# A Mamba and mixture-of-experts layer on one core: the places of its side work fitted anew

## The chip, the cores and the metric

The kernel runs on one core of a Trainium2 chip. The time is the device time of one execution in microseconds (us). Three executions of the kernel before took 4769.98, 4778.06 and 4780.16 us; the median is 4778.06. The engines are PE (TensorE), DVE (VectorE), ACT (ScalarE), POOL (GpSimd) and SP (SyncE, which here only issues transfers). Each runs its own list of instructions in order and waits on semaphores for the others.

## What is computed

```python
x = x + layernorm(mamba(layernorm(x)))        # x: 8 sequences, 1024 tokens, 256 channels
x = x + layernorm(moe(layernorm(x)))

# mamba, once forward and once on the reversed sequence, 512 channels, 16 states:
h = exp(delta * A) * h + (delta * B * x)       # one step a token
y = sum over states of h * C, + D * x, * silu(z)
# the two directions are added, halved, and go through W_out
# moe: a shared expert, and for each token the 2 best of 8 experts, gelu(t @ w1 + b1) @ w2 + b2
```

## The kernel before

The eight sequences are eight blocks. A block has two waves: w = 2b is the forward direction, w = 2b + 1 the backward one. A wave has 16 states times 4 groups of 128 channels, so 64 units, and the whole program 1024. A unit is one scan over 1024 tokens: ACT makes `decay` (PSUM, two buffers) with an Exp of `delta`, POOL makes `drive` (three buffers) from `xu` and a row of B, DVE scans both into `h`. PE transposes `h` into `h_t` by tiles of 128 tokens, and each tile is multiplied with C and added into `y`: twelve of sixteen tiles on DVE (L1118), four as `scaled` on ACT (L1328) and a sum on POOL (L1574).

The main loop of each engine goes over slots, two to a unit. In an even slot DVE does a scan, in each slot it may add one tile, and behind that come the pieces of side work whose place falls into the slot. A place is a number in the table AT, sixteen to a slot:

```python
def put(self, engine, at, piece, *index):
    self.slots[engine, at // PARTS].append((at, piece, index))
```

So slot 1024 is unit 512, the first of block 4. A slot is no time: an engine works its list as fast as its waits allow. Nothing checks that a piece that makes something stands in an earlier slot than the one that uses it on another engine; the semaphore then holds the second one up, and with it all that stands behind it on its engine.

The pieces of side work fall into three chains. *Preparing the next wave*: tok_load, norm, proj, xz_copy, the convolution as tap0 (ACT, L1357) and tap (DVE, L1181, three operations), silu_x (L1362), dbc_mm, then for each channel group c dt_mm, softplus (ACT, L1404 to L1408), delta (DVE, L1148), u_mul (POOL, L1588), delta_store and delta_load through DRAM (SP, L1756 and L1762). The `decay` of a wave's units of group c needs its delta_load. The backward wave's input comes back by xz_load (L1723), which waits for the last delta of the forward wave, as both use one buffer. *Finishing the block before*: y_dump, y_load (L1789), z_mm, z_copy and z_silu (L1420), y_turn, y_add, gate, out_mm, norms, residual. *Its experts*: routing on DVE (top1, top2, `slots`), scatter of the tokens on POOL (L1619, 16 indirect transfers for a block), for groups of four blocks of 128 tokens xs_load, xs_turn, r1_mm (L1073), r1_copy (L1518), a GELU (rgelu, L1524), r2_mm (L1081), ys_copy (L1536), ys_store (L1865), then gather on POOL (L1630, 16 transfers), comb_mm (L1058), comb (L1280), and the last norm: statistics, `ln_rstd` on POOL, ln_apply on ACT (L1449), fin_add (L1286), out_store. The experts of a block reach over the next block's units and into the one after; the gather stands at the start of that.

The side work's PSUM products share two banks. A second table, BANK_USE, numbers the uses; even numbers are one bank, odd ones the other, and a product waits for the piece that empties the use two numbers before it.

SP's list holds all hardware transfers in order, so one that waits holds up those behind it.

Of the kernel before, what the change touches and what calls it, by code (L numbers as in the profile page):

```python
# [1944 lines left out]
```

## Time and profile before

| | us |
|---|---|
| median of three executions | 4778.06 |
| the profiled execution | 4797.45 |
| its span | 4796.2 |
| before the first scan | 105.0 |
| scans, 1024 units | 4279.6 |
| from the last scan's start to the end | 411.5 |

The profiled execution is one of its own, so sums are made against its 4797.45. Busy shares of its span: DVE 83%, POOL 74%, PE 72%, ACT 62%. In the trace a row names the line of the program, the engine, what it writes and reads by the program's buffer names, and in square brackets how long the engine had stood idle before it and what ended that.

### The profile page before, as it was taken

The page shows a single profiled execution, that of the slowest core. Times are in us where ns is not written, and L with a number is a line of the kernel's source. Part 1 is how long each engine was busy: PE and PEld are TensorE (multiplying, and loading weights), DVE is VectorE, ACT ScalarE, POOL GpSimd, SP SyncE. Part 2 cuts the span into 40 slices and gives each one's busy share as a digit, 9 for nine tenths or more (in the row PEclk, how much of TensorE's full clock was granted, in tenths as well). Part 3 has the DMA queues.
Part 4 walks back from the last instruction along what each step waited for, and adds up shares of the span by engine and source line. Part 5 has one row for each costly group of instructions (what it writes and reads, how often), then busy time and mean ns, then how long its engine had stood idle before and what let it go on. Part 6 is the DMA issues. An engine that isn't in the chain of part 4 may idle for free.

```text
span 4796.2 us, 52660 instructions
## 1 busy us (share of the span) xinstructions
PE 3453.1 (72%) x16720; PEld 2505.7 (52%) x16720; DVE 3984.6 (83%) x4136; ACT 2979.6 (62%) x4196; POOL 3571.5 (74%) x2119
## 2 busy tenths in 40 slices
PE   4466767786777867887678867787678867787575
PEld 1344444665446644665456644566456655565354
DVE  2999998998989889799998989899997989896200
ACT  3454655775657756676657856677566756575243
POOL 2798887978877878778888878878887878786111
PEclk7565777998879878898779977898779988798687
DMA  4321331555325543456325543356424554255144
GB/s 130 106 79 66 110 128 71 184 180 178 129 96 189 180 152 120 144 184 204 129 91 176 196 157 132 123 179 215 142 84 166 174 194 137 94 186 162 62 157 148
DMA packets 362016, 687.42 MB, mean 143 GB/s; under 512 B 31873, under 2 KB 205450, under 8 KB 357642
## 3 DMA queue, kind: packets, MB, share of 16 engines
q1 hardware_dynamic: 349450, 650.48, 40.9%
q0 software_dynamic: 12288, 33.57, 2.2%
q8 instruction: 133, 2.18, 0.2%
q14 instruction: 145, 1.19, 0.1%
HBM read 513.04 MB, written 170.92 MB: 143 GB/s over the span
## 4 chain that ended last, share of the span: by engine, by line
DVE 31%; issue 18%; PE 17%; POOL 13%; ACT 12%; DMA 8%; SPq 1%; DVEq 0%; POOLq 0%; ACTq 0%
DVE h L1103 14%; DVE y L1118 9%; POOL drive L1566 7%; PE h_t L946 4%; PE side L1081 3%; DVE side L1181 3%; ACT decay L1310 2%; PE side L1051 2%; DMA expert_w<-in_w 2%; POOL y L1574 2%; POOL work L1630 2%; DVE stats L1162 1%; DMA ys_dram<-work 1%; PE side L1073 1%; DMA dx_dram<-prep_work 1%
## 5 line engine op out<-in xcount | busy, mean ns | idle before, releaser
L1566 POOL TENSOR_TENSOR drive<-xu,b_row 128x1024 f32<-128x1024 f32 x1024 | 2408.6, 2364 | 298.7 <-DVE h L1103 295.1
L1103 DVE TENSOR_TENSOR_SCAN h<-decay,drive 128x1024 f32<-128x1024 f32 x1024 | 2334.0, 2279 | 127.4 <-POOL drive L1566 85.4
L946 PE MATMUL h_t<-ident,h 128*128 128x128 f32 x8192 | 1511.2, 324 | 770.7 <-DVE y L1118 483.2
L946 PEld LDWEIGHTS h_t<-ident,h 128*128 128x128 f32 x8192 | 1128.0, 166 | 1261.0 <-DVE y L1118 714.0
L1310 ACT ACTIVATE decay<-delta,neg_a 128x1024 f32<-128x1024 f32 x1024 | 1141.5, 1117 | 789.6 <-DVE h L1103 736.9
L1118 DVE SCALAR_TENSOR_TENSOR y<-h_t,c_col,y 128x512 f32<-128x512 f32 x1488 | 1071.4, 734 | 147.8 <-PE h_t L946 139.0
L1574 POOL TENSOR_TENSOR y<-y,scaled 128x512 f32<-128x512 f32 x496 | 632.1, 1274 | 320.5 <-ACT scaled L1328 317.2
L1073 PE MATMUL side<-xn_t,expert_w 128*128 128x128 f32 x2944 | 415.3, 288 | 95.0 <-DMA expert_w<-in_w 26.7
L1081 PE MATMUL side<-expert_w,work 128*128 128x256 f32 x1472 | 405.3, 428 | 47.4 <-issue 29.6
L1073 PEld LDWEIGHTS side<-xn_t,expert_w 128*128 128x128 f32 x2944 | 378.2, 202 | 113.1 <-ACT work L1536 31.0
L1328 ACT ACTIVATE scaled<-h_t,c_col 128x512 f32<-128x512 f32 x496 | 339.8, 685 | 113.6 <-PE h_t L946 111.1
L1081 PEld LDWEIGHTS side<-expert_w,work 128*128 128x128 f32 x1472 | 307.0, 218 | 106.1 <-issue 38.0
L1630 POOL DMA_INDIRECT work<-ys_dram,slot_i x128 | 123.8, 967 | 254.7 <-DMA ys_dram<-work 224.3
L1280 DVE TENSOR_TENSOR acc<-side,acc 128x512 f32<-128x512 f32 x32 | 22.1, 690 | 287.4 <-PE side L1058 283.3
L1518 ACT ACTIVATE work<-side,b_blocks 128x128 f32<-128x128 f32 x736 | 208.1, 365 | 63.4 <-PE side L1073 63.1
L1181 DVE SCALAR_TENSOR_TENSOR side<-prep_work,chan_sb,side 128x512 f32<-128x512 f32 x256 | 191.8, 749 | 38.9 <-ACT side L1357 34.2
L1619 POOL DMA_INDIRECT xs_dram<-work,slot_i x128 | 125.5, 980 | 127.6 <-DVE owner_hot L1274 67.3
L1588 POOL TENSOR_TENSOR xu<-xu,prep_work 128x1024 f32<-128x1024 f32 x64 | 151.0, 2359 | 81.9 <-DVE prep_work L1148 81.6
L1058 PE MATMUL side<-work 128*128 128x256 f32 x256 | 113.9, 592 | 112.1 <-DMA work<-ys_dram,slot_i 85.8
L984 PE MATMUL side<-dbc,wdt_sb 97*128 97x512 f32 x256 | 171.8, 785 | 18.6 <-DVE prep_work L1148 9.0
L1051 PE MATMUL side<-expert_w,work 128*128 128x256 f32 x512 | 152.0, 450 | 35.7 <-ACT work L1472 31.4
L964 PE MATMUL side<-xn_t,w_in_sb 128*128 128x512 f32 x256 | 139.8, 677 | 28.6 <-DVE xu L1181 26.1
(148 smaller groups left out, 3730.0 us busy)
## 6 DMA issues: line engine op xcount, KB each, us to landing
expert_w<-in_w SPq DMA_DIRECT2D x384, 512.0 KB, 4.1
b_row<-b_dram SPq DMA_DIRECT2D x256, 512.0 KB, 4.4
dx_dram<-prep_work SPq DMA_DIRECT2D x64, 512.0 KB, 3.4
delta_dram<-prep_work SPq DMA_DIRECT2D x64, 512.0 KB
delta<-delta_dram SPq DMA_DIRECT2D x64, 512.0 KB, 3.6
work<-xs_dram SPq DMA_DIRECT2D x40, 512.0 KB, 4.8
ys_dram<-work SPq DMA_DIRECT2D x40, 512.0 KB, 5.4
xz_dram<-prep_work SPq DMA_DIRECT2D x32, 512.0 KB, 4.1
```

Source lines behind the costliest of these rows:

```text
L946: t = pe.e.transpose(h_t[i % N_H_T][:, c * P:(c + 1) * P], h[:, gn % 2, c, tb * P:(tb + 1) * P], ident[:, :])
L1051: pe.e.matmul(o, h1[:, m, q * P:(q + 1) * P], wo[:, m, :], start=(m == 0), stop=False)
L1073: mm = pe.e.matmul(bank[:, m * P:(m + 1) * P], wi[:, k, m * P:(m + 1) * P], xn2_t[:, k, at:at + P], start=(k == 0), stop=(k == DC - 1))
L1081: mm = pe.e.matmul(bank[:, q % 2 * D:(q % 2 + 1) * D], h1_blocks[:, q, m, :], wo[:, m, :], start=(m == 0), stop=(m == HC - 1))
L1103: dve.e.tensor_tensor_scan(o, a, v, 0.0, ALU.mult, ALU.add).then_inc(scanned, 1)
L1118: dve.e.scalar_tensor_tensor(out=y[:, tb, :], in0=h_t[i % N_H_T][:, :], scalar=c_n, in1=y[:, tb, :], op0=ALU.mult, op1=ALU.add).then_inc(s ...
L1181: op = dve.e.scalar_tensor_tensor(out=into, in0=xz_pad[:, at:at + BANK], scalar=chan_col(d, c, CHAN_CONV_W + k), in1=bank[:, :], op0=ALU.m ...
L1310: act.e.activation(decay[k % N_DECAY][:, :], delta[:, c, :], ACT.Exp, scale=neg_a[:, c, w % 2, n:n + 1]).then_inc(decay_made, 1)
L1328: act.e.mul(into, h_t[i % N_H_T][:, :], c_col[:, w % 2, tb, n:n + 1]).then_inc(tile_scaled, 1)
L1566: pool.e.tensor_tensor(drive[:, k % N_DRIVE, :], xu[:, w % 2, c, :], b_row[:, gn % N_B_ROW, :], ALU.mult).then_inc(drive_made, 1)
L1574: pool.e.tensor_tensor(y[:, tb, :], y[:, tb, :], scaled[:, at % N_SCALED, :], ALU.add).then_inc(gathered, 1)
L1630: pool.e.indirect_dma_start(out=found[:, tb % N_FOUND, r, :], out_offset=None, in_=ys_dram, in_offset=bass.IndirectOffsetOnAxis(ap=slot_i[ ...
```

## The change

The instructions are the same. The numbers in AT are other ones, and BANK_USE is numbered to fit. In the old table blocks 0, 1 and 2 each had places of their own, and blocks 3 to 6 those of one pattern; in the new one the pattern holds from block 1 on. One line of the table stands for all (scatter; 16 to a slot, eight places to a block):

```diff
-    "scatter": [5616, 5632, 5664, 5680, 5728, 5760, 5824, 5888, 10160, 10176, 10208, 10224, 10240, 10241, 10242,
+    "scatter": [5744, 5760, 5792, 5808, 5824, 5856, 5872, 5888, 9840, 9856, 9888, 9904, 9920, 9952, 9968, 9984,
```

Below, code lines after the change are higher by one (L1103 is L1104).

**The start of block 4, DVE.** L1148 is delta of the wave that just begins (channel group 3, the two halves of the tokens), L1181 the taps of the next wave, L1103 the scans of slots 1028 and so on; the last scan shown is the wave's first unit of group 3. Before:

```order
L1148 SCALAR_TENSOR_TENSOR prep_work<-side,prep_work 128x512
L1118 SCALAR_TENSOR_TENSOR y<-h_t,c_col,y 128x512
L1148 SCALAR_TENSOR_TENSOR prep_work<-side,prep_work 128x512
L1103 SCALAR_TENSOR_TENSOR h<-decay,drive 128x1024
L1118 SCALAR_TENSOR_TENSOR y<-h_t,c_col,y 128x512
L1103 SCALAR_TENSOR_TENSOR h<-decay,drive 128x1024
L1118 SCALAR_TENSOR_TENSOR y<-h_t,c_col,y 128x512 x2
L1181 SCALAR_TENSOR_TENSOR side<-prep_work,chan_sb,side 128x512 x2
L1181 SCALAR_TENSOR_TENSOR xu<-prep_work,chan_sb,side 128x512
L1103 SCALAR_TENSOR_TENSOR h<-decay,drive 128x1024
```

After:

```order
L1104 SCALAR_TENSOR_TENSOR h<-decay,drive 128x1024
L1119 SCALAR_TENSOR_TENSOR y<-h_t,c_col,y 128x512
L1104 SCALAR_TENSOR_TENSOR h<-decay,drive 128x1024
L1119 SCALAR_TENSOR_TENSOR y<-h_t,c_col,y 128x512 x2
L1149 SCALAR_TENSOR_TENSOR prep_work<-side,prep_work 128x512
L1182 SCALAR_TENSOR_TENSOR side<-prep_work,chan_sb,side 128x512 x2
L1182 SCALAR_TENSOR_TENSOR xu<-prep_work,chan_sb,side 128x512
L1182 SCALAR_TENSOR_TENSOR side<-prep_work,chan_sb,side 128x512 x2
L1182 SCALAR_TENSOR_TENSOR xu<-prep_work,chan_sb,side 128x512
L1104 SCALAR_TENSOR_TENSOR h<-decay,drive 128x1024
```

The second delta has moved from two scans ahead of that unit to directly ahead of it, and the first delta (not shown) from slot 1024 to 1018. Both taps of slot 1029 now stand behind it; before, one did.

**The same place, ACT.** L1310 is `decay`, L1404 to L1408 one softplus, L1536 ys_copy, L1357 tap0, L1524 and L1525 the GELU of the last expert group of block 2. Before:

```order
L1404 ACTIVATE prep_work<-side 128x512
L1406 ACTIVATE prep_work<-prep_work 128x512
L1408 ACTIVATE prep_work<-prep_work 128x512
L1310 ACTIVATE decay<-delta,neg_a 128x1024 x2
L1328 ACTIVATE scaled<-h_t,c_col 128x512
L1536 COPY work<-side 128x512
L1357 ACTIVATE side<-prep_work,chan_sb 128x512
L1310 ACTIVATE decay<-delta,neg_a 128x1024
```

After:

```order
L1329 ACTIVATE scaled<-h_t,c_col 128x512
L1525 ACT_TABLE_LOAD
L1525 ACTIVATE work<-work 128x1536
L1526 ACT_TABLE_LOAD
L1405 ACTIVATE prep_work<-side 128x512
L1407 ACTIVATE prep_work<-prep_work 128x512
L1409 ACTIVATE prep_work<-prep_work 128x512
L1537 COPY work<-side 128x512
L1358 ACTIVATE side<-prep_work,chan_sb 128x512
L1537 COPY work<-side 128x256
L1358 ACTIVATE side<-prep_work,chan_sb 128x512
L1311 ACTIVATE decay<-delta,neg_a 128x1024 x2
```

The last `decay` row begins with the one for group 3. Ahead of it there now stand a GELU, the softplus of the late delta, two ys_copies whose r2_mm stand in slots 1028 and 1030 of PE, and two tap0 that wait for xz_load. The first gather stands in slot 1028 of POOL, before in 1047.

**The scatter of block 3 within block 4, POOL.** L1619 is the scatter, L1566 `drive`, L1574 the sum of a `y` tile, L1588 u_mul. Before, from slot 1150:

```order
L1619 DMA xs_dram<-work,slot_i 3072x256 x2
L1574 TENSOR_TENSOR y<-y,scaled 128x512
L1619 DMA xs_dram<-work,slot_i 3072x256 x2
L1566 TENSOR_TENSOR drive<-xu,b_row 128x1024
L1619 DMA xs_dram<-work,slot_i 3072x256 x12
L1588 TENSOR_TENSOR xu<-xu,prep_work 128x1024
L1566 TENSOR_TENSOR drive<-xu,b_row 128x1024
L1574 TENSOR_TENSOR y<-y,scaled 128x512
L1566 TENSOR_TENSOR drive<-xu,b_row 128x1024 x2
```

After, from slot 1127:

```order
L1620 DMA xs_dram<-work,slot_i 3072x256 x2
L1567 TENSOR_TENSOR drive<-xu,b_row 128x1024
L1620 DMA xs_dram<-work,slot_i 3072x256 x2
L1567 TENSOR_TENSOR drive<-xu,b_row 128x1024
L1620 DMA xs_dram<-work,slot_i 3072x256 x2
L1575 TENSOR_TENSOR y<-y,scaled 128x512
L1620 DMA xs_dram<-work,slot_i 3072x256 x2
L1567 TENSOR_TENSOR drive<-xu,b_row 128x1024
L1620 DMA xs_dram<-work,slot_i 3072x256 x2
L1567 TENSOR_TENSOR drive<-xu,b_row 128x1024
L1620 DMA xs_dram<-work,slot_i 3072x256 x2
L1575 TENSOR_TENSOR y<-y,scaled 128x512
```

Twelve transfers in a row with u_mul behind them have become eight pairs over ten slots; u_mul follows two `drive` later.

**After the last scans, SP.** L1780 is y_dump of the last block, L1865 the store of block 6's last expert group, L1839 the load of an expert's weights, L1815 x1_load, L1799 dx_half_load, L1789 y_load. Before:

```order
L1839 DMA expert_w<-in_w 128x4x256
L1780 DMA y_dram<-y 128x512 x2
L1839 DMA expert_w<-in_w 128x2x512
L1780 DMA y_dram<-y 128x512 x6
L1839 DMA expert_w<-in_w 128x4x256
L1815 DMA work<-x_dram 128x2048
L1865 DMA ys_dram<-work 128x3x256
L1799 DMA work<-dx_dram 128x512 x2
L1789 DMA work<-y_dram 128x4x512
```

After:

```order
L1840 DMA expert_w<-in_w 128x4x256
L1840 DMA expert_w<-in_w 128x2x512
L1840 DMA expert_w<-in_w 128x4x256
L1816 DMA work<-x_dram 128x2048
L1866 DMA ys_dram<-work 128x3x256
L1781 DMA y_dram<-y 128x512 x8
L1800 DMA work<-dx_dram 128x512 x2
L1790 DMA work<-y_dram 128x4x512
```

The store stood behind all y_dumps and now stands ahead of them (slot 2046, before 2068), as do on PE its r2_mm (slot 2044, before 2066). The gather of block 6 stands in slots 2061 to 2071, before 2070 to 2082; nothing else of POOL's lies between its last `y` sum and that gather in either. On ACT ln_apply of block 6 (slots 2080 to 2082) now stands ahead of z_silu (2083), before behind it (2095 and 2092). On PE rank_mm of block 7 goes behind both mix_turns. All other pieces of block 7 behind y_load keep their order on each engine.

On ACT, in the last quarter of each block, silu_x, four r1_copy, a GELU and four dx_mul stood in slots 1215 to 1235 of block 4 and stand in 1226 to 1239.

## Rows read from the trace of the kernel before

**Rows 1.** Windows: stretch: its us, busy us of each engine (instructions), clock, DMA

```profile
2214.70:2761.50 546.80, 415.65 (x2091) 304.46 (x2090) 498.32 (x518) 371.43 (x525) 445.80 (x259) 0.84 0.47 156
...
4384.70:4796.20 411.50, 251.94 (x1031) 183.67 (x1030) 49.36 (x142) 135.71 (x250) 68.80 (x75) 0.76 0.39 124
```

**Rows 2.** Waits of DVE, third quarter of block 4: us, times, longest

```profile
DVE y L1118 <- PE h_t L946: 9.4, 7, 2.2
```

**Rows 3.** Timeline, start of block 4: start us, us, engine, line [idle before]

```profile
2214.71 2.29 DVE L1103 TENSOR_TENSOR_SCAN h<-decay,drive 128x1024 f32<-128x1024 f32 x1 [0.40 <-ACT decay L1310]
...
2220.28 0.68 DVE L1148 SCALAR_TENSOR_TENSOR prep_work<-side,prep_work 128x512 f32<-128x512 f32 x1
...
2233.70 1.12 ACT L1310 ACTIVATE decay<-delta,neg_a 128x1024 f32<-128x1024 f32 x1 [6.32 <-DMA delta<-delta_dram]
...
2234.85 2.29 DVE L1103 TENSOR_TENSOR_SCAN h<-decay,drive 128x1024 f32<-128x1024 f32 x1 [4.21 <-ACT decay L1310]
```

**Rows 4.** Windows, first to fourth scan: block 2; sum of blocks 3 to 7

```profile
1123.70:1133.50 9.80, 6.29 (x48) 5.30 (x48) 9.80 (x9) 6.39 (x14) 9.38 (x6) 1.00 0.65 217
...
sum 95.01, PE 71.92 PEld 54.63 DVE 67.64 ACT 46.01 POOL 71.09; mean PE 14.38 PEld 10.93 DVE 13.53 ACT 9.20 POOL 14.22
```

**Rows 5.** Timeline of DVE, start of block 0

```profile
124.95 1.29 DVE L1148 SCALAR_TENSOR_TENSOR prep_work<-side,prep_work 128x512 f32<-128x512 f32 x2 [13.81 <-DMA delta_dram<-prep_work]
...
132.73 1.55 DVE L1181 SCALAR_TENSOR_TENSOR side<-prep_work,chan_sb,side 128x512 f32<-128x512 f32 x2 [0.95 <-ACT side L1357]
...
137.22 4.46 DVE L1103 TENSOR_TENSOR_SCAN h<-decay,drive 128x1024 f32<-128x1024 f32 x2
```

**Rows 6.** Groups of block 4: count | busy us, mean ns | idle before

```profile
L1566 POOL TENSOR_TENSOR drive<-xu,b_row 128x1024 f32<-128x1024 f32 x128 | 301.3, 2366 | 35.8 <-DVE h L1103 35.6
...
L1310 ACT ACTIVATE decay<-delta,neg_a 128x1024 f32<-128x1024 f32 x129 | 143.8, 1117 | 89.3 <-DVE h L1103 82.1 <-DMA delta<-delta_dram 6.3 <-issue 0.4
...
L1518 ACT ACTIVATE work<-side,b_blocks 128x128 f32<-128x128 f32 x92 | 26.0, 364 | 4.2 <-PE side L1073 4.2
...
L1524 ACT ACTIVATE work<-work 128x1536 f32<-128x1536 f32 x1 | 1.5, 1483 | 0.0
...
L1524 ACT ACT_TABLE_LOAD x6 | 7.7, 1283 | 0.1
...
L1362 ACT ACTIVATE xu<-xu 128x4096 f32<-128x4096 f32 x1 | 3.6, 3629 | 0.0
```

**Rows 7.** Timeline of POOL and DVE, scatter of block 4

```profile
2500.26 1.09 POOL L1619 DMA_INDIRECT xs_dram<-work,slot_i  x1 [5.62 <-DVE owner_hot L1274]
...
2514.52 0.96 POOL L1619 DMA_INDIRECT xs_dram<-work,slot_i  x1 [2.05 <-issue]
...
2532.30 2.29 DVE L1103 TENSOR_TENSOR_SCAN h<-decay,drive 128x1024 f32<-128x1024 f32 x1 [11.40 <-POOL drive L1566]
...
2557.50 2.28 DVE L1103 TENSOR_TENSOR_SCAN h<-decay,drive 128x1024 f32<-128x1024 f32 x1
```

**Rows 8.** Waits of DVE, last quarter of block 4

```profile
DVE h L1103 <- ACT decay L1310: 0.8, 2, 0.4
```

**Rows 9.** Timelines of POOL, ACT and SP after the last scan

```profile
4392.89 1.26 POOL L1574 TENSOR_TENSOR y<-y,scaled 128x512 f32<-128x512 f32 x1 [1.66 <-ACT scaled L1328]
...
4414.10 1.01 POOL L1630 DMA_INDIRECT work<-ys_dram,slot_i  x1 [19.96 <-DMA ys_dram<-work]
...
4444.36 0.20 POOL L1604 TENSOR_TENSOR shift<-shift,rstd 128x8 f32<-128x8 f32 x1
...
4450.45 4.00 ACT L1449 ACTIVATE side<-acc,shift,rstd 128x256 f32<-128x256 f32 x8
...
4455.26 0.37 SPq L1789 DMA_DIRECT2D work<-y_dram  x1
```

**Rows 10.** Timeline of DVE, routing of block 4

```profile
2482.39 0.23 DVE L1134 TENSOR_TENSOR cand<-cand,rank 128x64 f32<-128x64 f32 x1
...
2485.99 2.25 DVE L1134 TENSOR_TENSOR cand<-cand,rank 128x64 f32<-128x64 f32 x1
```

More of the change, by code:

```diff
@@ new lines @@
+    "tok_stats": [-2176, -2175, -1856, -1840, 2560, 2576, 2720, 2736, 6304, 6368, 6672, 6688, 10400, 10464, 10768,
+        10784, 14496, 14560, 14864, 14880, 18592, 18656, 18960, 18976, 22688, 22752, 23056, 23072, 26784, 26848,
+        27152, 27168],
+    "tok_var": [-2160, -1824, 2608, 2752, 6480, 6704, 10576, 10800, 14672, 14896, 18768, 18992, 22864, 23088, 26960,
+        27184],
+    "tok_rstd": [-2000, -1808, 2624, 2784, 6496, 6720, 10592, 10816, 14688, 14912, 18784, 19008, 22880, 23104,
+        26976, 27200],
@@ new lines @@
+    "z_copy": [3232, 3248, 3568, 3600, 4768, 4784, 4848, 4880, 8560, 8592, 8608, 8624, 9040, 9072, 9074, 9105,
[4 rows of a table added]
+    "z_silu": [3696, 4912, 8625, 9120, 12721, 13216, 16817, 17312, 20913, 21408, 25009, 25504, 29105, 29600, 33328,
+        33681],
+    "y_dump": [4112, 4128, 4160, 4161, 4176, 4192, 4224, 4225, 8208, 8224, 8280, 8281, 8282, 8283, 8352, 8353,
[4 rows of a table added]
+    "y_load": [4193, 4513, 8736, 8864, 12832, 12960, 16928, 17056, 21024, 21152, 25120, 25248, 29216, 29344, 33328,
+        33441],
+    "y_turn": [4304, 4368, 4464, 4528, 4576, 4880, 5056, 5104, 8768, 8769, 8832, 8848, 8896, 9104, 9184, 9200,
[4 rows of a table added]
@@ new lines @@
+    "mix_turn": [5680, 5696, 9776, 9792, 13872, 13888, 17968, 17984, 22064, 22080, 26160, 26176, 30256, 30272,
+        34256, 34272],
+    "rank_mm": [5697, 9793, 13889, 17985, 22081, 26177, 30273, 34273],
+    "slots": [5696, 9792, 13888, 17984, 22080, 26176, 30272, 34288],
+    "bias_mm": [5714, 9810, 13906, 18002, 22098, 26194, 30290, 34336],
+    "gelu": [5729, 6000, 9825, 10096, 13921, 14192, 18017, 18288, 22113, 22384, 26209, 26480, 30305, 30576, 34320,
+        34576],
+    "bias_copy": [5730, 9826, 13922, 18018, 22114, 26210, 30306, 34368],
@@ L512 @@
+    "xs_turn": [183, 185, 187, 189, 195, 160, 205, 170, 229, 231, 204, 206, 310, 312, 314, 316, 322, 361, 332, 371,
[19 rows of a table added]
+    "comb_mm": [234, 269, 271, 273, 435, 396, 398, 400, 562, 597, 599, 601, 763, 724, 726, 728, 890, 925, 927, 929,
+        1091, 1052, 1054, 1056, 1182, 1219, 1184, 1221, 1319, 1290, 1321, 1292],
 }
```

294 lines of the change are left out of this document (134 added, 160 removed), and 617 rows, old and new, of tables (AT, BANK_USE).

## The prediction

> **What bounds the kernel now.** I read the split of the span first. In one block of the middle DVE works 498.32 us of 546.80; POOL has 445.80, PE 415.65, ACT 371.43 [rows 1]. So the scan's engine sets the pace, and what can be won there is its idle time, some 48 us a block. After the last scan come 411.50 us in which DVE works 49.36 [rows 1]: that part is a chain through all engines, and only what that chain holds matters. The waits of DVE, taken by quarter of a block, then say where its 48 us go: in the third quarter 11.4 us for one `drive` of POOL and 9.4 us for PE's transposes [rows 2, 7]; at a block's start for ACT's `decay`; the rest in pieces of 1 to 3 us. So I look at four places: the end, the block starts, the scatter, and the load between them.
>
> **The end of the scans: -24 us.** The instructions are the same, so every gain is order. Before, r2_mm of block 6's last group, ys_copy and ys_store stand behind the last transposes, and the first gather starts at 4414.10, 19.96 us idle after POOL's last `y` ended (4392.89 + 1.26 = 4394.15) [rows 9]. In the change that store is issued ahead of all y_dumps and its r2_mm is done five transposes before the end, so gathers start where POOL's last `y` ends: -19.9 us. Next, ACT so far does z_silu (two table loads of 1.28 and a pass over 2048 columns, 1.9 if the 1.48 of 1536 columns is scaled [rows 6]: 4.5 us) before the four ln_apply, which start at 4450.45, though POOL's last operation for them ends at 4444.36 + 0.20 = 4444.56 [rows 9]. In the change ln_apply stands ahead of z_silu; of the 5.9 us between the two I count 4.4, as the last z_copy still stands among them. z_silu then lies beside the y_load that so far waited for it. Together -24.3. Behind y_load (4455.26 [rows 9]) all engines keep the order of block 7's pieces but for one: rank_mm goes behind two mix_turns. It makes the scatter some 2 us later, and xs_load has more slack than that; nothing.
>
> **The block starts: +26 us.** Three scans before unit 3 of a block, `decay` needs delta of channel group 3, which goes DVE, store, load, ACT. Block 4 before: delta ends at 2220.28 + 0.68 = 2220.96, `decay` starts at 2233.70, the scan at 2234.85, after 4.21 us of waiting [rows 3]. So delta to scan is 13.9 us. In block 0, with a quieter DMA, the same trip lay inside delta end 126.24 to scan 137.22, 11.0 us, of which 6.5 were the wait for xz_load until the first tap and 4.5 the two taps [rows 5]. In the change the last delta moves from slot 1025 to 1029, one slot ahead of the scan that needs it; only the two taps are left between. Its ACT piece stands behind a GELU. From the start of scan 512: the scan 2.28, `decay` 1.12, r1_copy 4 x 0.365, four passes over 512 columns (`scaled` and the three of softplus) at some 0.6, half of what `decay` takes for 1024, the GELU with its table loads 1.48 + 2 x 1.28, delta 0.68: 12.0 us [rows 3, 6]. Then 11.0 to 13.9: the fourth scan starts 23.0 to 25.9 after the first, I take 24. Before, five blocks took 95.01 together, 19.0 each, and block 2, placed otherwise, 9.80 [rows 4]. But work moved in: the window held 67.64 / 5 = 13.5 us of DVE work [rows 4] and now holds 1.6 more (one delta less, one tap more); in block 2 it held only its own 9.80 and now 5.2 more. So 5 x (24 - 19.0 - 1.6) + (24 - 9.8 - 5.2) = 17 + 9 = 26 us. Block 1 keeps its delta well ahead. The gathers now stand four slots behind that trip, and the first waits for the store of the group that ys_copy feeds, itself behind a tap0. I cost them at nothing: POOL's wait lies beside DVE's own, and both orders give POOL about the same lump, 16 transfers in 10 to 13 slots. Bounds -3 to +4 a block.
>
> On the trip the Trainium skill ("DMA: Bandwidth & Descriptors", Latency and other measured facts) says that HBM access takes 0.2 us on average and 2 us at high load. By that each of the two transfers could be up to 1.8 us slower than in quiet block 0, so the trip 11.0 + 3.6 = 14.6, an estimate; the rows show 13.9 under load [rows 3]. Taken so, the block starts would cost some 3 us more each.
>
> **The scatter: -30 us.** Before, two pairs and then twelve transfers in a row stand in POOL's program, with u_mul right behind, at the very start of the block's second half. From the first transfer (2500.26) the scan that needs the next `drive` waits until 2532.30, 11.40 us idle [rows 7], and the twelfth scan after that first transfer starts at 2557.50, 57.2 us after the first transfer [rows 7]. The lump also pays 2.05 us of "issue" twice, of which the row of one is shown [rows 7]. In the change the eight pairs stand in ten slots with a `drive` between each two, and u_mul two scans later. A pair costs 2 x (0.97 + 0.30) = 2.54, a `drive` 2.37, a `y` 1.26 [rows 6, 7, 9]. Laid end to end POOL makes the twelfth `drive` so that its scan starts 47.6 us after the first transfer; DVE has three drives in hand and waits some 10 us in four pieces. Before, the same stretch also held tok_stats and tok_var, 3.8 us, which now lie elsewhere: 57.2 - 3.8 - 47.6 = 5.8. I take 5 (1.7 if both "issue" waits stay) for six blocks (block 0 was spread already): -30.
>
> **The rest: +3 us.** PE carries eo_mm, xs_turn and r1_mm more thinly behind the scatter; of 9.4 us of waits for transposes [rows 2] some 5.9 lie inside POOL's lump and go with it, of the other 3.5 I take 2, six times: -12. Against that silu_x (3.63 + 2 x 1.28 [rows 6]), four r1_copy, a GELU and four dx_mul now stand within 14 slots of ACT, where they had 21. ACT's work there exceeds DVE's by some 8 us, before by some 5, of which the whole quarter shows 0.8 us of waits for `decay` [rows 8]. I take +2.5, six times: +15. Bounds 0 and 6.5.
>
> **Sum.** -24 + 26 - 30 - 12 + 15 = -25 us, on the profiled execution's 4797.45. The runs shown have a median of 4778.06, so 4753. This measurement can tell 0.2%, 9.6 us, from no change.
>
> **Rivals.**
> 1. *The block start knots further (slower).* ys_copy stands four slots ahead of its r2_mm, tap0 behind a load that waits for the late delta, `decay` behind both. If the gap of four scans is 30 us and not 24, six blocks cost 36 more: 4789. It decides from some 28 us on. For it: ACT already sat idle 6.32 us for this load [rows 3]. Against: in block 0 the same order ran in 11.0.
> 2. *ACT's lump is paid in full (no change).* At 6.5 instead of 2.5, six times, +24: 4777. For it: ACT has only two PSUM buffers of `decay` ahead. Against: before, an excess of 5 us cost under 1 [rows 8].
> 3. *PE's relief and the spread scatter give more.* All of 3.5 on PE and 8 on POOL: -9 - 18, so 4726. For it: POOL lost 4.1 us to "issue".
> 4. *The lock.* DVE's little operations on two SBUF inputs beside POOL's: L1134 takes 0.23 and 2.25 us in one block [rows 10]. The kernel's routing has five such, so their excess of some 6 us a block could be nothing or 12: -40 to +40 over seven blocks, to either side, by the phase of POOL's `drive`. I see no move of `drive` against them and cost it at nothing, chance 0.04. The Trainium skill ("SBUF — State Buffer", Who interferes with whom) says so: DVE and GpSimd hold a shared port pair exclusively for a whole instruction. The rows agree, 2.25 being one `drive` of 2.37.
>
> **Chances.** Forecast 0.48, rival 1 0.18, rival 2 0.17, rival 3 0.13, rival 4 0.04. Its own range is 4735 to 4768. Over all the range reaches from rival 3 with ACT's term halved (-8) to rival 1 with half a us more a block start (+3): 4718 to 4792. Faster by over 0.2%: nearly all of the forecast and rival 3, 0.59; within 0.2%: rival 2 and the edge of the forecast, 0.19; slower: most of rival 1 and part of the others, 0.22.
>
> **What would show it.** The profile of the changed kernel should have: the first gather of the end right behind POOL's last `y`, and from that `y` to y_load some 37 us where it was 61.1; 23.0 to 25.9 us from scan 0 to scan 3 of blocks 2 to 7, with DVE idle ahead of taps and scan; no single wait of 11 us for `drive`, but several of 2 to 4; fewer waits for h_t in the third quarter; in the fourth, waits of 2 to 4 us for `decay`. Wrong would make me: a fourth scan over 28 us late, gathers that start that trip's length later and starve `drive`, or a blocked `decay` in the last quarter.

## The result, and the profile after

The changed kernel took 4737.44 us (median of 4 runs, 4736.2 to 4744.18), the kernel before 4779.11 us beside it (4769.98 to 4786.84): a ratio of 0.9913 with a 95% interval of 0.9898 to 0.9929, so 0.9% faster. A second set of runs of the same kernel (after_again) gave 0.9911 (0.9893 to 0.9929). The forecast was 4753 us, 25 less; it is 42 less in the medians. The profiled execution of the changed kernel lasted 4736.2 us, near its median, where that of the kernel before lay 18 us above its own; between the two profiles the difference is 61 us, and the account below is of these 61.

The split of the span, block 4 and the part after the last scan, and then block 4 by quarter (columns as in [rows 1]). Changed kernel:

```profile
2195.44:2741.60 546.16, 404.89 (x2093) 296.50 (x2092) 497.31 (x519) 370.47 (x525) 445.52 (x259) 0.86 0.47 157
4351.53:4735.00 383.47, 240.89 (x1008) 176.30 (x1006) 49.38 (x142) 130.52 (x245) 68.66 (x75) 0.78 0.41 130
...
2195.44:2354.20 158.76, 101.91 (x440) 70.82 (x438) 137.24 (x145) 95.43 (x123) 120.85 (x75) 0.77 0.46 156
2354.20:2506.50 152.30, 109.83 (x472) 75.28 (x470) 131.65 (x168) 88.25 (x120) 122.63 (x77) 0.78 0.28 95
2506.50:2623.30 116.80, 95.52 (x601) 74.84 (x600) 115.70 (x112) 87.38 (x140) 103.58 (x59) 0.99 0.56 185
2623.30:2741.60 118.30, 97.62 (x587) 75.56 (x587) 112.72 (x98) 99.41 (x144) 98.46 (x50) 0.97 0.64 208
```

Against [rows 1], 546.80 and 411.50: the end lost 28.0 us, a block of the middle 0.6. By quarter block 4 took 148.6, 140.1, 144.4 and 113.7 us before. Those quarters don't compare one by one, since side work moved out of the third into the first and second; only their sum does. TensorE's granted clock (the last column but two) differs too: in the third quarter it is 0.99, and 0.94 in the same quarter of the kernel before:

```profile
2503.39:2647.75 144.36, 120.35 (x648) 89.90 (x647) 122.43 (x121) 100.37 (x152) 116.13 (x73) 0.94 0.55 182
```

The waits of DVE over the whole of block 4 (us, times, longest), kernel before:

```profile
DVE y L1118 <- PE h_t L946: 18.3, 15, 2.2
DVE h L1103 <- POOL drive L1566: 11.6, 2, 11.4
DVE h L1103 <- ACT decay L1310: 6.1, 6, 4.2
DVE acc L1280 <- PE side L1058: 4.9, 3, 3.1
```

and changed:

```profile
DVE h L1104 <- POOL drive L1567: 18.7, 11, 5.6
DVE y L1119 <- PE h_t L947: 8.3, 11, 1.5
DVE side L1182 <- ACT side L1358: 7.5, 1, 7.5
DVE logits L1212 <- PE side L1016: 2.5, 1, 2.5
DVE h L1104 <- ACT decay L1311: 2.0, 3, 0.8
```

The waits were exchanged, not removed: transposes and `decay` 14 us less, `drive` 7 more, a tap0 7 more. DVE's idle time in block 4 is 48.5 us before and 48.9 after. Where the 61 us are, from the starts of the scans in both traces:

| part | before | after | difference |
|---|---|---|---|
| before the first scan | 105.0 | 103.6 | -1.4 |
| block 0, 1, 2 | 489.4, 529.3, 542.1 | 483.2, 516.3, 546.1 | -6.2, -13.0, +4.0 |
| blocks 3 to 6 | 548.9, 546.8, 550.0, 552.7 | 546.2, 546.1, 546.1, 548.2 | -11.8 together |
| block 7 to its last scan | 520.5 | 515.7 | -4.8 |
| after the last scan | 411.5 | 383.5 | -28.0 |

### The profile page after: what moved, and what is told of

It reads as the page before. It is cut to its first block, busy times and chain, and to the rows that moved or that the text cites. A ratio compares the mean times of both kernels' runs of the same rounds, so it can differ in the third digit from the quotient of the medians.

```text
span 4735.0 us, 52683 instructions
## 1 busy us (share of the span) xinstructions
PE 3366.6 (71%) x16720; PEld 2441.2 (52%) x16720; DVE 3978.3 (84%) x4136; ACT 2975.1 (63%) x4196; POOL 3570.4 (75%) x2119
## 4 chain that ended last, share of the span: by engine, by line
DVE 36%; POOL 21%; issue 21%; ACT 9%; PE 8%; DMA 4%; SPq 0%; DVEq 0%; POOLq 0%; ACTq 0%
DVE h L1104 17%; POOL drive L1567 12%; DVE y L1119 10%; DVE side L1182 3%; POOL y L1575 3%; POOL xs_dram L1620 2%; POOL work L1631 2%; ACT decay L1311 2%; DVE stats L1163 1%; POOL xu L1589 1%; PE h_t L947 1%; PE side L1082 1%; ACT work L1525 1%; ACT scaled L1329 1%; ACT work L1519 1%
## 5 line engine op out<-in xcount | busy, mean ns | idle before, releaser
L1104 DVE TENSOR_TENSOR_SCAN h<-decay,drive 128x1024 f32<-128x1024 f32 x1024 | 2332.4, 2278 | 148.1 <-POOL drive L1567 121.7
L947 PE MATMUL h_t<-ident,h 128*128 128x128 f32 x8192 | 1472.0, 318 | 852.2 <-DVE y L1119 544.6
L947 PEld LDWEIGHTS h_t<-ident,h 128*128 128x128 f32 x8192 | 1092.6, 162 | 1355.9 <-DVE y L1119 807.3
L1082 PE MATMUL side<-expert_w,work 128*128 128x256 f32 x1472 | 400.8, 424 | 69.1 <-issue 34.6
L1074 PE MATMUL side<-xn_t,expert_w 128*128 128x128 f32 x2944 | 388.5, 277 | 38.9 <-DVE xu L1182 14.8
L1074 PEld LDWEIGHTS side<-xn_t,expert_w 128*128 128x128 f32 x2944 | 355.0, 192 | 50.7 <-DVE xu L1182 17.7
L1620 POOL DMA_INDIRECT xs_dram<-work,slot_i x128 | 126.3, 987 | 114.3 <-DVE owner_hot L1275 68.6
L985 PE MATMUL side<-dbc,wdt_sb 97*128 97x512 f32 x256 | 161.2, 734 | 13.2 <-DVE prep_work L1149 5.9
L1059 PE MATMUL side<-work 128*128 128x256 f32 x256 | 104.8, 551 | 70.6 <-DMA work<-ys_dram,slot_i 54.1
L1003 PE MATMUL side<-w_out_sb,work 128*128 128x256 f32 x512 | 137.4, 419 | 21.8 <-POOL work L1611 14.5
```

The costliest lines, as they stand in the source:

```text
L947: t = pe.e.transpose(h_t[i % N_H_T][:, c * P:(c + 1) * P], h[:, gn % 2, c, tb * P:(tb + 1) * P], ident[:, :])
L1074: mm = pe.e.matmul(bank[:, m * P:(m + 1) * P], wi[:, k, m * P:(m + 1) * P], xn2_t[:, k, at:at + P], start=(k == 0), stop=(k == DC - 1))
L1082: mm = pe.e.matmul(bank[:, q % 2 * D:(q % 2 + 1) * D], h1_blocks[:, q, m, :], wo[:, m, :], start=(m == 0), stop=(m == HC - 1))
L1104: dve.e.tensor_tensor_scan(o, a, v, 0.0, ALU.mult, ALU.add).then_inc(scanned, 1)
L1620: pool.e.indirect_dma_start(out=xs_dram, out_offset=bass.IndirectOffsetOnAxis(ap=slot_i[:, r, tb:tb + 1], axis=0), in_=tokens[:, tb, :], i ...
```

## The experiments

Names: a_ is a variant of the changed kernel, b_ one of the kernel before. A place divided by 16 is the slot; the diffs show block 4's numbers, and the other blocks of the pattern have the same plus or minus 4096. "First gather" and "twelfth scan" are counted from the block's first scan, here block 4.

| run | median us | ratio to before (95%) | first gather | twelfth scan |
|---|---|---|---|---|
| the changed kernel | 4737.4 | 0.9913 (0.9898 to 0.9929) | 27.3 | 68.5 |
| again (after_again) | 4737.0 | 0.9911 (0.9893 to 0.9929) | 27.8 | 69.0 |
| a_delta | 4747.7 | 0.9927 (0.9910 to 0.9944) | 28.7 | 70.0 |
| a_gelu | 4750.4 | 0.9940 (0.9924 to 0.9955) | 29.6 | 70.9 |
| a_free | 4754.9 | 0.9945 (0.9925 to 0.9964) | 30.9 | 72.1 |
| a_lump | 4784.4 | 1.0000 (0.9988 to 1.0013) | 28.0 | 69.2 |
| a_ys | 4700.5 | 0.9832 (0.9816 to 0.9849) | 21.4 | 63.5 |
| a_ys_act | 4734.7 | 0.9913 (0.9891 to 0.9934) | 27.7 | 68.9 |
| a_wide | 4706.4 | 0.9854 (0.9830 to 0.9878) | 20.8 | 62.1 |
| b_tail | 4767.3 | 0.9967 (0.9951 to 0.9984) | | |
| b_head | 4780.9 | 0.9997 (0.9984 to 1.0009) | | |
| b_spread | 4786.5 | 1.0007 (0.9993 to 1.0021) | | |
| b_spread2 | 4783.8 | 1.0004 (0.9991 to 1.0016) | | |

> The changed kernel unaltered, as the measure for the other runs of this call and of the one before. Both theories: a ratio of 0.991 to 0.993 to the kernel before; on this chip it should show how much of the difference between the changed kernel and its variants is the chip's.

### The end alone (b_tail)

```diff
-"ys_store" (6,5): 33089    "rgelu" (6,5): 32960    "r2_mm" (6,20..22): 32992, 33040, 33056
+"ys_store" (6,5): 32912    "rgelu" (6,5): 32736    "r2_mm" (6,20..22): 32768, 32832, 32848
-"gather" (6,0..7): 33120, 33152, 33184, 33200, 33232, 33264, 33280, 33312
+"gather" (6,0..7): 32976, 33008, 33040, 33056, 33072, 33104, 33120, 33136
```

> The kernel before, with only the end of the program in the changed order: the last expert group of block 6 and its store ahead of block 7's y_dumps, and everything from slot 2046 on (gather, ln_apply, z_silu, block 7's finish and experts) at the places of the change. Theory (the step of the end, on its own): from the last scan's start to the end 383 to 387 us where it was 411.5, so 24 to 28 us less than the kernel before, a ratio of about 0.9945. Rival (the end only gains because the last wave before it also carries less): at most half, 12 to 14 us, a ratio of 0.997.

It took 18.6 us less by the medians, 8 to 23 by the ratio, where the theory had 24 to 28; the interval holds the rival's 0.997 and not the theory's 0.9945. So the ratio doesn't decide it, and the trace has to. POOL's timeline, first of b_tail, whose last scan starts at 4378.00:

```profile
4390.40 1.27 POOL L1574 TENSOR_TENSOR y<-y,scaled 128x512 f32<-128x512 f32 x1 [2.83 <-ACT scaled L1328]
4398.25 1.01 POOL L1630 DMA_INDIRECT work<-ys_dram,slot_i  x1 [6.58 <-DMA ys_dram<-work]
```

then of the changed kernel, whose last scan starts at 4351.53, with SP's y_load:

```profile
4360.68 1.26 POOL L1575 TENSOR_TENSOR y<-y,scaled 128x512 f32<-128x512 f32 x1 [1.66 <-ACT scaled L1329]
4362.09 1.01 POOL L1631 DMA_INDIRECT work<-ys_dram,slot_i  x1
```

```profile
4398.43 0.37 SPq L1790 DMA_DIRECT2D work<-y_dram  x1
```

In b_tail the last expert group stands some ten slots later than in the changed table, so its store lands later and the gather starts 20.2 us after the last scan, not 10.6. From the last scan to the end it has 392.8 us where the changed kernel has 383.5: the 9.3 us are the 9.6 by which the gather is late. So between these two kernels the start of the gather passes to the end of the program at full price. With that correction the theory accounts for the end: the order alone shortens it from 411.5 to 392.8 us, and the rest of the change shortens it to 383.5.

### The scatter (a_lump, b_spread, b_spread2, a_wide)

a_lump puts the changed kernel's scatter together, b_spread spreads that of the kernel before:

```diff
 a_lump
-"scatter" (3,0..7): 18032, 18048, 18080, 18096, 18112, 18144, 18160, 18176
+"scatter" (3,0..7): 18032, 18048, 18080, 18081, 18082, 18082, 18082, 18082
 b_spread
-"scatter" (3,0..7): 18400, 18416, 18432, 18433, 18434, 18435, 18436, 18437
+"scatter" (3,0..7): 18400, 18416, 18432, 18464, 18480, 18512, 18528, 18544
```

> The changed kernel, with the scatter of blocks 1 to 6 put together again: two pairs in their own slots and twelve transfers in a row in slot 1130 (of block 4), where the change has eight pairs over ten slots; u_mul stays. Theory (the step of the scatter: spreading saves 5 us a block): 30 us slower, about 4767 us, with one wait for drive of 11 us and more. Rival (POOL has the same work to do up to the twelfth drive in either order, and DVE waits as long in one piece as in several): 4737 to 4747, the waits for drive in that quarter staying at 11 us in sum.

> The kernel before, with only the scatter of blocks 1 to 6 laid over ten slots, as the change does, at its own place in the program; all else stays. Theory (the lump costs what the run that lumped it in the changed kernel gave back, 7 to 8 us a block, or the 5 of my sum): 30 to 45 us less than before, a ratio of 0.991 to 0.9935. Rival (in the order before, u_mul and the drives behind the scatter bind as much, and the spread transfers only move the wait): a ratio of 0.998 to 1.000.

Waits of DVE in the scatter's quarter of block 4, a_lump:

```profile
DVE h L1104 <- POOL drive L1567: 14.2, 1, 14.2
DVE y L1119 <- PE h_t L947: 6.1, 6, 2.6
DVE prep_work L1149 <- ACT prep_work L1409: 2.0, 2, 1.7
```

In the changed kernel that quarter has 11.0 us for `drive` in five waits of at most 5.6. The lump costs 3.2 there, 2.4 in transposes, 1.7 for softplus; the block takes 555.7 us where it took 546.1. So spreading is worth 47 us in the changed kernel by the medians, 42 by the ratios, more than my 30; the rival, by which it would cost nothing, falls. In the kernel before it is worth nothing. Its third quarter with the scatter spread:

```profile
DVE y L1118 <- PE h_t L946: 12.7, 11, 2.9
DVE stats L1162 <- DMA prep_work<-in_x: 7.3, 1, 7.3
```

The 11.4 us for `drive` [rows 7] are gone, and 7.3 for tok_load and 3.3 more for transposes [rows 2] stand in their place. tok_stats waits for tok_load. By the program tok_load waits for the u_mul behind the scatter, but in this trace that u_mul ends at 2513.45, and the transfer stands on SP behind a load of expert weights, which waited 8.9 us for the shared expert's first product on PE (L1041):

```profile
2511.10 2.35 POOL L1588 TENSOR_TENSOR xu<-xu,prep_work 128x1024 f32<-128x1024 f32 x1 [1.80 <-DVE prep_work L1148]
```

```profile
SPq L1837 <- PE side L1041: 8.9, 1, 8.9
```

```profile
2523.56 0.40 SPq L1839 DMA_DIRECT2D expert_w<-in_w  x1
2524.01 0.47 SPq L1694 DMA_DIRECT2D prep_work<-in_x  x1
```

So both waits that stand in the place of `drive` lead back to PE. b_spread2 moves tok_stats three slots on as well (and tok_var, tok_rstd, the first tok_apply):

```diff
-"tok_stats" (5,0): 18544, 18560    "tok_var": 18561
+"tok_stats" (5,0): 18592, 18608    "tok_var": 18609
```

> The kernel before with the scatter spread as in the run that gained nothing, and beside it the token statistics of the next block but one (tok_stats, tok_var, tok_rstd of the first half, blocks 4 to 7) three slots later on DVE, as the trace of that run shows DVE waiting 7.3 to 9.4 us there for tok_load where it waited 11 us for drive before. Theory (spreading pays only with this second wait out of the way): four blocks gain 7 us and more each, 25 to 35 us less than before, a ratio of 0.993 to 0.9955. Rival (PE, busy 136 of that quarter's 147 us, is the third in the row: waits for h_t grow by what the other wait loses): a ratio of 0.998 to 1.001.

```profile
DVE y L1118 <- PE h_t L946: 16.2, 12, 3.1
DVE h L1103 <- POOL drive L1566: 4.4, 1, 4.4
```

The rival holds: now the transposes take 16.2. The quarter has POOL's wait and PE's standing one behind the other. What the change did there is to take other work out of it (in block 4 PE's busy time in the third quarter falls from 120.4 to 95.5 us, DVE's from 122.4 to 115.7), which only the whole table does; that this is what makes the spreading pay is argued from the three runs, not tried by itself. Last, a_wide goes the other way, from a_ys (below):

```diff
-"scatter" (3,0..7): 18032, 18048, 18080, 18096, 18112, 18144, 18160, 18176
+"scatter" (3,0..7): 18032, 18064, 18096, 18128, 18176, 18208, 18256, 18288
```

> The kernel with both exchanges (4700 us), and the scatter of blocks 1 to 6 laid wider: eight pairs over 16 slots where the change has ten. Theory (POOL has 28 us of slack in that quarter and DVE waits 10.9 us for drives there, so what is spread lies beside DVE): the waits for drive fall to 3 to 5 us, 6 to 8 us a block, 36 to 48 in all: about 4660 us. Rival (as in the kernel before, the next wait stands right behind: u_mul, tok_load, or PE's transposes): less than 10 us, 4690 to 4700, with a new wait in that quarter.

```profile
DVE h L1104 <- POOL drive L1567: 11.8, 5, 3.5
```

My theory fell. The sum is 11.8 where a_ys has 11.0, and only the longest piece shrinks, from 5.1 to 3.5; the median is 4706 against 4700, with ratios whose intervals overlap. The wait that the rival asked for, a new one in that quarter, isn't there either: the waits for `drive` simply stay. POOL's slack, some 30 us over the quarter, doesn't lie where the scatter is. With the transfers that far apart they meet the next u_mul in slot 1140; that this is what keeps the sum up I have not tried.

### The block starts (a_delta, a_gelu, a_free)

```diff
 a_delta
-"dt_mm" (8,3,1): 16400    "softplus": 16417    "delta": 16464    "delta_store" (8,3): 16465
+"dt_mm" (8,3,1): 16377    "softplus": 16385    "delta": 16400    "delta_store" (8,3): 16415
 a_gelu
-"softplus" (8,3,1): 16417    "rgelu" (2,5): 16416
+"softplus" (8,3,1): 16416    "rgelu" (2,5): 16417
 a_free: as a_delta (but "delta_store" 16414), and
-"xz_load" (4,0): 16466    "delta_load" (8,3): 16468    "tap0" (9,0): 16419, 16421    "tap": 16465, 16466
+"xz_load" (4,0): 16432    "delta_load" (8,3): 16448    "tap0" (9,0): 16464, 16482    "tap": 16496, 16512
```

> The changed kernel, with the last dt_mm, softplus, delta and delta_store of the forward waves of blocks 2 to 7 four slots earlier, ahead of the GELU; nothing else moves. Theory (the late delta is the price of the block starts): the fourth scan starts 17 to 19 us after the first instead of 23.9, and 5 to 6 us a block come back, 30 to 36 in all: about 4704 us. Rival (POOL bounds that stretch, as its gather pairs between the drives make 1.2 us of waiting a scan right behind): what DVE gains up to the fourth scan it gives back as waits for drive up to the eighth, and the kernel takes 4727 to 4737.

> The changed kernel, with only two neighbours on ACT exchanged at the start of blocks 2 to 7: the softplus of the late delta now stands ahead of the GELU with its two table loads. Theory: delta ends 4.0 us earlier and the fourth scan starts at 20 us instead of 23.9, six times 4 is 24: about 4713 us. Rival (the drives behind the gathers take it back, or the taps then wait for tap0, which still stands behind the GELU and ys_copy): 4730 to 4737, with the wait for tap0 as long as before.

Neither is faster, and both forecasts failed. The fourth scan of block 4 starts 24.3 and 25.9 us after the first, where I had said 17 to 19 and 20 and the changed kernel has 23.9. By the medians they are 10 and 13 us slower than the changed kernel, slower than their rivals said too; by the ratios 7 and 13, with intervals that overlap its own. SP's timeline shows why the earlier delta doesn't help, here a_delta:

```profile
2208.23 0.34 SPq L1757 DMA_DIRECT2D delta_dram<-prep_work  x1
2208.63 0.42 SPq L1781 DMA_DIRECT2D y_dram<-y  x1
2210.41 6.79 SPq L1840 DMA_DIRECT2D expert_w<-in_w  x2
2217.24 0.47 SPq L1724 DMA_DIRECT2D prep_work<-xz_dram  x1
2219.78 0.37 SPq L1840 DMA_DIRECT2D expert_w<-in_w  x1
2220.26 0.45 SPq L1763 DMA_DIRECT2D delta<-delta_dram  x1
```

The two loads of expert weights ahead of xz_load occupy the queue for 6.8 us, as the second waits for a buffer that r2_mm frees, and r2_mm waits for the GELU. The changed kernel has this wait too (from 2200.39 to 2207.46), but there the late delta ends only at 2207.31, so it doesn't show. In a_gelu the GELU comes later, and the two loads hold the queue for 9.1 us. The GELU, r2_mm and that load were a second chain as long as mine. a_free takes them out of the way:

> The changed kernel, with the late delta four slots earlier and the transfers that the two earlier variants showed in its way moved too: on SP xz_load and delta_load stand ahead of the load of expert weights that waits for r2_mm of block 2's last group, on ACT the two tap0 stand two to four slots later, on DVE the two taps three to six slots later, behind the fourth scan. Theory (what fixes the fourth scan in the changed kernel is the GELU, r2_mm, that load in SP's queue and then xz_load; freed of it delta comes after the store and the load alone): the fourth scan starts 15 to 17 us after the first where it was 23.9, of which 4.5 are the two taps that now come later; 3 to 4 us a block remain, 18 to 24 in all, if POOL lets them. Rival (POOL's gathers, which start only when ys_store has landed, set the pace from there): the twelfth scan after the first stays at 67 to 70 us and the kernel within 5 us of the changed one.

Its scans 0 to 3 of block 4 took 20.28 us (I had said 15 to 17, for `decay` stood behind the ys_copy), 3.6 less than the changed kernel's, and yet the twelfth scan starts 72.1 after the first (70.0 to 70.5 in the other five blocks) and the kernel is 18 us slower, where the rival had allowed 5. The table above has the rule: in the changed kernel and these variants the twelfth scan starts 41.2 to 41.3 us after the first gather, whatever the fourth does. From the first gather on POOL has eight pairs and its drives to make and is the engine that sets the pace; the fourth scan isn't what counts. The kernels' times follow: over blocks 2 to 7 the first gathers stand 163.3 us behind their blocks' starts in sum in the changed kernel, and 172.9, 178.2 and 176.0 in the three variants, 10, 15 and 13 more, for medians 10, 13 and 18 us up. The windows from scan 0 to scan 12, kernel before and changed:

```profile
2214.71:2269.82 55.11, 40.15 (x206) 32.66 (x204) 46.26 (x42) 33.44 (x49) 36.98 (x19) 0.80 0.69 230
```

```profile
2195.44:2263.95 68.51, 39.80 (x175) 29.51 (x174) 49.12 (x47) 33.81 (x51) 48.92 (x33) 0.75 0.54 184
```

DVE's idle time there grows from 8.9 to 19.4 us, POOL's work from 37.0 to 48.9.

### What releases the gather (a_ys, a_ys_act)

If that is so, an earlier ys_store pays. In the changed kernel its ys_copy stood behind a tap0, and it itself behind delta_load:

```diff
-"ys_copy" (2,22): 16420    "ys_store" (2,5): 16471    "delta_load" (8,3): 16468    "x1_load": 16469    "b_row_load" (130): 16470
+"ys_copy" (2,22): 16418    "ys_store" (2,5): 16468    "delta_load" (8,3): 16469    "x1_load": 16470    "b_row_load" (130): 16471
```

a_ys_act has the new place of ys_copy alone.

> The changed kernel, with two exchanges at the start of blocks 2 to 7: on ACT the last ys_copy stands ahead of the tap0 that waits for xz_load, and on SP ys_store stands ahead of delta_load. Nothing else moves. In the changed kernel r2_mm ends at 2211.36, but that ys_copy starts only at 2214.73, behind tap0. Theory (POOL sets the pace of a block's start from the first gather on: in the four kernels so far, whatever the fourth scan did, the twelfth scan after the first started 41.2 to 41.4 us after the first gather): the gather starts 3.3 us earlier, at 24.0 instead of 27.3 us, the twelfth scan at 65.3, six times 3.3 is 20: about 4717 us. Rival (the fourth scan, held by xz_load and delta_load, sets the pace): the twelfth scan stays at 68 and the kernel at 4733 to 4740.

> The changed kernel with only the first of the two exchanges of the last run: the last ys_copy ahead of the tap0 that waits for xz_load; ys_store stays behind delta_load on SP. Theory (the queue of SP is the larger part: with both exchanges ys_store landed 4.9 us after its issue where the changed kernel shows 7.6, and was issued 5.6 us earlier after the block's first scan): ys_store is issued when delta_load, x1_load and b_row_load are out, 1.2 us earlier than in the changed kernel, its landing stays at 7.6 us, the gather starts at 26 us, 7 us less in all: about 4730 us. Rival (ACT's order is what counts, and SP's exchange only follows): the gather starts at 22 to 23 us, and the kernel takes 4700 to 4710.

a_ys is the fastest kernel of this study, 1.7% under the kernel before and 37 us under the changed one, where I had expected 20. Its six first gathers stand at 127.3 us in sum, 36.0 less than the changed kernel's. a_ys_act gains nothing. SP and POOL in the changed kernel (first scan of the block 2195.44):

```profile
2212.70 0.32 SPq L1763 DMA_DIRECT2D delta<-delta_dram  x1
2213.11 0.38 SPq L1816 DMA_DIRECT2D work<-x_dram  x1
2213.54 0.42 SPq L1770 DMA_DIRECT2D b_row<-b_dram  x1
2215.11 0.37 SPq L1866 DMA_DIRECT2D ys_dram<-work  x1
```

```profile
2222.71 1.06 POOL L1631 DMA_INDIRECT work<-ys_dram,slot_i  x1 [7.03 <-DMA ys_dram<-work]
```

in a_ys_act (2196.07):

```profile
2214.82 0.43 SPq L1866 DMA_DIRECT2D ys_dram<-work  x1
```

```profile
2223.78 1.06 POOL L1631 DMA_INDIRECT work<-ys_dram,slot_i  x1 [7.45 <-DMA ys_dram<-work]
```

and in a_ys (2189.51):

```profile
2205.93 0.37 SPq L1866 DMA_DIRECT2D ys_dram<-work  x1
2206.94 0.33 SPq L1763 DMA_DIRECT2D delta<-delta_dram  x1
```

```profile
2210.91 1.06 POOL L1631 DMA_INDIRECT work<-ys_dram,slot_i  x1 [1.14 <-DMA ys_dram<-work]
```

From issue to gather the store takes 7.6, 9.0 and 5.0 us. In the first two it stands behind delta_load, x1_load and b_row_load, and issuing it 0.9 us earlier (18.75 against 19.67 after the first scan) doesn't make it land earlier. a_free shows the same: its store is issued at 19.7 behind two loads of expert weights, x1_load and b_row_load, and takes 11.1 us. In a_ys, ahead of the three loads, it is issued at 16.4 and lands at 21.4. So the exchange on ACT is worth nothing by itself, and with the one on SP the two make 3.3 us of earlier issue and 2.6 to 4 of faster landing; I had counted only the first. SP's exchange alone was not tried; without the other it would have the whole queue wait for ys_copy. In a_ys the twelfth scan comes 42.1 us after the first gather in block 4, where DVE now waits 5.0 us for comb_mm, and 41.2 to 41.3 in the other five.

### The first blocks alone (b_head)

```diff
-every place below 7584 (slot 474) of the table before
+every place below 7584 of the changed table
```

> The kernel before, with the changed places for everything below slot 474 (block 0 and the first 109 of block 1's 128 units); both tables have done the same pieces there. In the two traces unit 237 starts 940.9 and 933.2 us after the first scan. Theory (the gain of the first two blocks is real and lies in ACT's and PE's waits there): 7 to 8 us less than before, a ratio of 0.9984. Rival (it is a difference of two executions): no difference, 1.000. A ratio alone can hardly tell these apart, the start of unit 237 in the trace can.

From the first scan to unit 237 in the kernel before, in the changed one of the second set of runs, and in b_head:

```profile
105.05:1045.92 940.87, 634.20 (x2810) 445.38 (x2810) 882.51 (x844) 564.98 (x719) 763.39 (x413) 0.72 0.35 116
```

```profile
103.64:1037.69 934.05, 618.06 (x2804) 430.83 (x2805) 882.14 (x845) 563.32 (x717) 765.10 (x413) 0.74 0.35 115
```

```profile
106.13:1039.12 932.99, 615.14 (x2804) 427.91 (x2805) 882.01 (x844) 564.06 (x718) 766.00 (x413) 0.74 0.35 116
```

DVE's work is the same within 0.5 us, so the 7.9 us are waits that went: the traces of b_tail and b_spread show 940.9 and 941.0 there. The theory holds up to unit 237. The ratio of the whole, 0.9997, doesn't show them; its interval reaches to 0.9984, which is what they would make.

## Why the forecast came out as it did

**The end, -24.** Measured -28.0. The first gather starts 10.6 us after the last scan where it was 29.4, and y_load at 46.9 where it was 70.6: 23.7 less, for 24.3 forecast. The gather's start is 18.8 of this (19.9 forecast), the way from there to y_load the other 4.9 (4.4 forecast, for ln_apply ahead of z_silu). From POOL's last `y` to y_load it is 36.5 us, as said (some 37). The other 4.3 lie behind y_load, where I had put nothing; which wait they are is open. Other variants with this order have 329 to 337 us behind y_load, the kernels with the old order 340 to 341, so the sign at least repeats.

**The block starts, +26.** The part forecast was met: the fourth scan of blocks 2 to 7 starts 23.2 to 24.2 us after the first (forecast 24). The six windows grew by 142.6 - 104.7 = 37.9 us in sum, DVE's work in them by 89.7 - 77.4 = 12.4, so 25.5 net for 26. What went wrong is the next step: "I cost them at nothing", of the gathers, with bounds of -3 to +4. In block 4 DVE's idle time from scan 0 to scan 12 grew by 10.5 us, of which 2.3 up to the fourth scan; the other 8 or so stand behind it, where POOL makes the pairs and DVE waits for `drive`. The forecast had named gathers that "starve `drive`" as a sign that would make it wrong. Nor was delta the only chain to the fourth scan. The gathers had cost something in their old place too, waits of 4.9 us for comb_mm. Over the first quarters of the six blocks DVE's idle time grew by 43.7 us (table below), so 18 more than the 26 of this term.

**The scatter, -30.** The size was near; what failed is that the term stands by itself. The stretch that the forecast added up, from the first transfer to the twelfth scan behind it, took 57.2 us in block 4 before and 50.1 after, where 47.6 was forecast. DVE's work in it is 38.4 and 37.6 us, so the 3.8 taken off for tok_stats and tok_var should have been 0.8. Its idle time fell from 18.9 to 12.5: 6.4 for 5 (6.3 to 10.4 in blocks 3 to 6). a_lump has 57.3 and 20.0 idle, b_spread 58.2 and 19.2: undone alone the spreading costs 47 us, done alone it gives nothing. "DVE waits some 10 us in four pieces" was right (five waits, 11.0, one of them 5.6 where I had said 2 to 4), but the waits for `drive` were 11.4 before, so nothing went from that row: what went was the waits behind it.

**PE, -12.** "Of the other 3.5 I take 2": the waits for h_t fell from 18.3 to 8.3 us a block, and in the third quarter to 1.1. This and the scatter are one effect, which b_spread and b_spread2 show from one side and a_lump from the other. Together the two terms had 42 us; in the second and third quarters of the six blocks DVE's idle time fell by 46.7. So the sum was met and the division wrong: the waits for `drive` are 67 us there before and 65 after, those for h_t 71 and 26.

**ACT's lump, +15.** Nothing of it: DVE's waits for `decay` in the last quarter stay at 0.8 us [rows 8].

```profile
DVE y L1119 <- PE h_t L947: 4.5, 5, 1.5
DVE h L1104 <- ACT decay L1311: 0.8, 1, 0.8
```

Rival 2 falls. The excess of ACT's work over DVE's, 8 us by the forecast's count, is absorbed here as the 5 were, and over the six blocks DVE's idle time in the last quarter fell by 7.0.

**Left out.** Blocks 0 and 1 gained 19 us where I had nothing. I had read the steady pattern and taken the first two blocks for the same; b_head shows 8 of it on its own. And of the lock of rival 4 nothing shows: DVE's busy time of block 4 is 498.3 and 497.3 us.

**The sum.** Between the two profiled executions the forecast of -25 stands against -61. Of the 36 missing, 19 are blocks 0 and 1, 4 the end, 1 the time before the first scan, and 12 the blocks 2 to 7, where I had -1 (+26 - 30 - 12 + 15) and the scans show -12.6. Those blocks by quarter, DVE's idle time summed over the six:

| quarter of blocks 2 to 7 | idle before | idle after | difference | forecast |
|---|---|---|---|---|
| first | 86.3 | 129.9 | +43.7 | +26 |
| second and third | 173.0 | 126.3 | -46.7 | -42 |
| last | 40.5 | 33.5 | -7.0 | +15 |
| all | 299.8 | 289.8 | -10.0 | -1 |

DVE's work in them is 2.6 us less, which makes the 12.6. That these blocks come within 12 us of the forecast is luck: the start was priced 18 us too low, the last quarter 22 too high.

How much of the 12.6 is the change is open. The kernel before varies there: b_head, whose places in blocks 2 to 7 are those of before, took 3249.7 us for them, the profiled execution of the kernel before 3261.0, the two of the changed kernel 3248.3 and 3246.5. Against b_head the blocks 2 to 7 gained 1 to 3 us, against the kernel before 13 to 15, and the profiled execution of the kernel before is 18 us over its median. In the steady blocks 3 to 6 I had also read the one that ran best, 546.8 us where their mean is 549.6; the others wait longer for h_t or for `drive`. The third quarters of blocks 2 to 6 last from 142.7 to 149.9 us in the trace of before, those of the changed kernel 116.8 to 117.1. The runs show the same: 4766 to 4799 us in 23 executions of the kernel before, 4735 to 4744 in ten of the changed one.

What makes the quarter vary stays open. One thing goes with it: TensorE's granted clock. In the third quarters of blocks 3 to 6 it stood at its lower level (1.2 GHz) for 16 to 21 us before and for some 3.4 after, and over blocks 2 to 7 PE's busy time for the same instructions fell from 2462 to 2410 us. In the longest of these quarters, block 6, a stretch around the scatter ran wholly at the lower level, and in the 8 us behind it DVE waited 2.75 and 2.93 us for h_t; in block 4 the same stretch was mostly at the upper level, and DVE waited once, 1.5 us. The first row is block 6, the second block 4:

```profile
3626.40:3636.60 10.20, 9.18 (x22) 6.29 (x22) 7.50 (x12) 4.40 (x4) 10.20 (x6) 0.50 0.62 197
2530.90:2541.10 10.20, 10.01 (x42) 6.79 (x41) 8.77 (x14) 3.23 (x4) 10.20 (x6) 0.84 0.53 155
```

So part of the fall in the waits for h_t may have come through the clock. No run here changes the one without the other.

The sign and the range held, on the strength of the end, which was read rightly; in the blocks, errors of opposite sign cancelled.

## What to carry to other kernels

Where several engines' work crowds into one stretch, the waits can stand in line behind each other: here removing the longest alone gave nothing, and putting it back into a layout that had got rid of the others cost 47 us, so price such edits by undoing one in the finished layout as well as by doing one in the old. Follow a delayed step to the stretch's end, not to the first instruction that needs it: here the fourth scan could be moved 3.6 us without any gain, while the store that releases the gathers decided the block's start. And read the in-order DMA queue ahead of every transfer that something waits for: issuing a 384 KB store ahead of 2 MB of loads instead of behind them, once a block, together with an earlier ys_copy, took 37 us off, and the earlier ys_copy alone took none.

## What the runs showed of the hardware

The landing of ys_store was set by what stood ahead of it in the queue, not by its issue. Behind delta_load, x1_load and b_row_load (128x1024, 128x2048 and 128x1024 in four bytes, 2.1 MB by their shapes) ys_store took 7.6 and 9.0 us from issue to gather, ahead of them 5.0. The core's DMA moved 261 GB/s from scan 0 to scan 3 there, at which 2.1 MB are 8.0 us, an estimate: the three loads, issued at 2212.70 to 2213.96, would be through at about 2221, and the gather started at 2222.71. The Trainium skill ("DMA: Bandwidth & Descriptors", Queues, rings and completion order) says that each engine takes the descriptors of a ring in order; the traces agree with it, as far as the landing of this store shows.

The waiting for `drive` right behind the gathers came in pieces of 1.1 to 1.25 us, at five scans in a row in block 4: a drive and a pair of gathers on POOL make 4.8 us a unit, and the three drive buffers did not cover it.

```profile
2245.49 2.29 DVE L1104 TENSOR_TENSOR_SCAN h<-decay,drive 128x1024 f32<-128x1024 f32 x1 [1.24 <-POOL drive L1567]
```
